# First attention of a four-layer kernel: the next pair's projections and values inside this pair's key tiles, and cross maxima in row tiles

## The reference, cut to what matters

```
# layer 0: first attention, 16 heads of 64
q = layernorm(x) @ Wq * 64 ** -0.5
k, v = split(media @ Wkv)                         # media: 1601 x 128
attn = softmax(where(mask, q @ k.T, min))         # 256 x 1601 for each head
x = x + tanh(attn_gate) * ((attn @ v) @ Wo)
x = x + tanh(ff_gate) * (gelu(layernorm(x) @ W1) @ W2)
# layer 1: memory attention; layer 2: self attention, cross attention, MLP
cq = rms_norm(h) @ cq_w; ck, cv = split(ctx @ ckv_w)   # 16 heads of 8
h = h + (softmax(cq @ ck.T / sqrt(8)) @ cv) @ cdense_w
# layer 3: memory attention
```

## Time and profile before

| | us |
|---|---|
| median of 3 runs | 2678.3 (2676.37 to 2683.85) |
| the profiled execution, its own time | 2683.99 |
| its span, first to last instruction | 2682.2 |
| one batch (start of one to start of the next) | 665.5 |

### The profile page before, as it was taken

One profiled execution on the slowest core, in us unless ns is written; L12 is line 12 of the kernel. 1 busy time (PEld: TensorE's weight loads), 2 busy tenths in 40 slices (PEclk: granted clock), 3 DMA queues, 4 the chain that ended last, 5 costly groups with the idle time before them and its releaser, 6 DMA issues.

```text
span 2682.2 us, 37982 instructions
## 1 busy us (share of the span) xinstructions
PE 2143.2 (80%) x12540; PEld 1575.9 (59%) x12540; DVE 1572.0 (59%) x2513; ACT 851.2 (32%) x1530; POOL 467.2 (17%) x412
## 2 busy tenths in 40 slices
PE   4999776878599977687859997768876999686987
PEld 3677565546477666554747766655464776565545
DVE  6777346653677735665377763566437776355643
ACT  2444111441244412054124441205412443120531
POOL 2444010000244401000034440100003443010000
PEclk7999877899699988798969998869896999886988
DMA  4000101001000010100100001010011000101000
GB/s 153 13 4 32 67 1 71 1 1 40 30 9 4 32 67 1 71 1 1 40 29 9 4 32 67 1 71 1 1 40 30 9 4 32 67 1 71 1 1 4
DMA packets 15563, 74.54 MB, mean 28 GB/s; under 512 B 2096, under 2 KB 3760, under 8 KB 11952
## 3 DMA queue, kind: packets, MB, share of 16 engines
q1 hardware_dynamic: 14256, 68.90, 6.9%
q10 hardware_dynamic: 1152, 3.67, 0.3%
HBM read 71.51 MB, written 1.05 MB: 27 GB/s over the span
## 4 chain that ended last, share of the span: by engine, by line
PE 72%; DVE 17%; issue 7%; ACT 3%; DMA 1%; POOL 0%; DVEq 0%; SPq 0%; ACTq 0%; POOLq 0%
PE x L623 26%; PE st L623 22%; PE pv L623 18%; PE mi L623 4%; DVE rstd_work L1142 1%; DVE prob_sums L1425 1%; DVE max_parts L1245 1%; PE x L642 1%; DVE k_hi_lo L1142 1%; DVE recip_sum L1296 1%; DVE cq_blocks L1480 1%; DVE rstd_work L1201 1%; ACT probs L508 1%; ACT k_hi_lo L466 1%; DVE max_parts L1472 1%
## 5 line engine op out<-in xcount | busy, mean ns | idle before, releaser
L508 ACT ACTIVATE probs<-st 128x512 f32<-128x512 f32 x416 | 229.6, 596 | 385.3 <-PE st L623 380.6
L1472 DVE TENSOR_REDUCE max_parts<-x 128x1 f32<-128x832 f32 x256 | 253.8, 1021 | 109.2 <-PE x L623 107.6
L1245 DVE TENSOR_REDUCE max_parts<-x 128x1 f32<-128x832 f32 x256 | 258.7, 1017 | 54.6 <-PE x L623 53.2
L602 ACT ACTIVATE probs<-st 128x512 f32<-128x512 f32 x416 | 226.3, 596 | 189.0 <-PE st L623 186.4
L623 PE MATMUL st<-q_hi_hi,k_hi_lo 128*128 128x256 f32 x832 | 236.8, 315 | 28.9 <-ACT v L474 14.3
L431 POOL TENSOR_TENSOR prob_sums<-prob_sums,probs 128x512 f32<-128x512 f32 x160 | 205.6, 1285 | 250.0 <-ACT probs L508 250.0
L623 PE MATMUL pv<-probs,v 128*64 128x256 f32 x1664 | 223.2, 393 | 0.0
L623 PEld LDWEIGHTS st<-q_hi_hi,k_hi_lo 128*128 128x128 f32 x832 | 160.7, 193 | 104.2 <-issue 68.4
L623 PE MATMUL st<-q_lo_shift,k_hi_rows 128*128 128x256 f32 x832 | 213.1, 287 | 0.0
L395 POOL TENSOR_SCALAR k_hi_rows<-probs,const_cols 64x1664 fp32r<-64x1664 f32 x16 | 26.4, 1658 | 996.1 <-DVE probs L1209 995.8
L1142 DVE TENSOR_TENSOR prob_sums<-prob_sums,probs 128x512 f32<-128x512 f32 (+1 forms) x168 | 155.2, 924 | 75.0 <-ACT probs L528 42.9
(11 more groups left out here) (260 smaller groups left out, 4405.8 us busy)
## 6 DMA issues: line engine op xcount, KB each, us to landing
w_gate_up<-in_wgu SPq DMA_DIRECT2D x4, 3072.0 KB, 10.5
w_pair<-in_w SPq DMA_DIRECT2D x32, 256.0 KB, 2.7
w_ff<-in_w SPq DMA_DIRECT2D x8, 1024.0 KB, 5.8
w_qk<-in_wqk SPq DMA_DIRECT2D x4, 2048.0 KB, 9.1
w_down<-in_wdn SPq DMA_DIRECT2D x4, 1536.0 KB, 13.8
w_dense<-in_wd SPq DMA_DIRECT2D x4, 1024.0 KB, 12.5
mask_ints<-in_mask SPq DMA_DIRECT2D x4, 832.0 KB, 4.6
ctx_t_raw<-in_ctxT SPq DMA_DIRECT2D x4, 832.0 KB, 6.2
```

The costliest lines, as they stand in the source:

```text
L508: act.activation(prob[:, kt % 4], ST[kt % 2][:], ACT.Exp, scale=HD0 ** -0.5).then_inc(p_exp.handle, 1)
L602: act.activation(prob[:, n % 4], ST[n % 2][:], ACT.Exp, scale=float(HC2) ** -0.5)\
L1245: dve.tensor_reduce(mxs[:, qt, h, half:half + 1], X[half][:].rearrange("p (c n) -> p c n", c=2)[:, :, 0:QUART], AX.XY, ALU.max).then_inc(m ...
L1472: dve.tensor_reduce(mxs[:, qt, h, half:half + 1], X[half][:].rearrange("p (c n) -> p c n", c=2)[:, :, 0:QUART], AX.XY, ALU.max).then_inc(m ...
```

## The change

- `prep_q` and `prep_k` of pair p + 1 (not p + 2) are issued inside pair p, behind the scores of key tiles 0 to 3. Only pair 0 is prepared ahead of the loop.
- The values of two pairs (a "duo") are made at once: the moving operand has 256 columns, a `prep_v` tile is two key tiles into `MI`, there are 7 of them per duo. Four lie in the even pair and three in the odd pair ahead of the duo. The first duo's are made ahead of the loop.
- The maximum parts move from key tiles 2 to 9 to tiles 4 to 11, half 0 of the keys first. The transposed maxima go through `MI`.
- The sum of exponentials and the normalisation of pair p move behind the first two score tiles of pair p + 1. ScalarE copies `PV` to `attn` first (a new operation of 128 x 256), VectorE then multiplies in SBUF.
- VectorE adds three times per pair (tiles 5 and 7, 9, 11) instead of six tiles in five additions, GpSimd eight times instead of six.
- The pairs are written out instead of looped; the weights of a pair come in one buffer of 3 x 128 columns plus one of 256 columns per duo.
- In the second cross attention a maximum part is two heads x 416 keys instead of one head x 832 keys, and its two matmuls use only the 32 rows of their head.

The core of the diff (`...` marks what is left out; the ScalarE, GpSimd and SyncE parts follow the same order):

```diff
+DUOS = PAIRS // 2
+VT = -(-KT // 2)
+VS = 4
+ADD_DVE = (5, 7, 9, 11)
+ADD_POOL = tuple(kt for kt in range(KT) if kt not in ADD_DVE)
...
+        def v_tile(p, k0):
+            if p >= PAIRS - 2 or k0 < 2:
+                return None
+            c = k0 // 2 - 1 if p % 2 == 0 else VS + k0 // 2 - 1
+            return (p // 2 + 1, c) if c < (VS if p % 2 == 0 else VT) else None
...
@@ block.gpsimd: pair
+                    for n, kt in enumerate(ADD_POOL[1:]):
+                        pool.wait_ge(p_exp.handle, p_exp.at(i, kt + 1))
+                        if n == 0:
+                            pool.wait_ge(sum_mm.handle, sum_mm.at(i, 0))
+                            pool.tensor_tensor(acc[:, 0], prob[:, 0], prob[:, 1], ALU.add).then_inc(add_pool.handle, 1)
...
+                                queries(i + 1, 1 - p % 2)
+                                keys(i + 1, 1 - p % 2, 0)
...
+                        if kt == 3 and p < PAIRS - 1:
...
+                            keys(i + 1, 1 - p % 2, 1)
@@ block.scalar: pair
+                    for k0 in range(0, KT, 2):
+                        for kt in range(k0, min(k0 + 2, KT)):
+                            probs(kt)
+                        if p < PAIRS - 1 and k0 == 0:
+                            queries(i + 1, 1 - p % 2)
+                            keys(i + 1, 1 - p % 2, 0)
+                        if p < PAIRS - 1 and k0 == 2:
+                            keys(i + 1, 1 - p % 2, 1)
+                        if v_tile(p, k0):
+                            values(*v_tile(p, k0), MI)
+                    act.wait_ge(pv_mm.handle, pv_mm.at(i))
+                    act.activation(attn[:, p], PV[:, 0:NT], ACT.Copy).then_inc(pv_out.handle, 1)
@@ block.tensor: pair
                     for k0 in range(0, KT, 2):
                         for kt in range(k0, min(k0 + 2, KT)):
                             scores(kt)
-                        if not last_pair and 2 <= k0 < 10:
-                            max_part(i + 1, 1 - s, k0 - 2)
-                            max_part(i + 1, 1 - s, k0 - 1)
+                        if k0 == 0 and p:
+                            sums(i - 1)
+                        if p < PAIRS - 1:
+                            if k0 == 0:
+                                prep_q(i + 1, 1 - s, False)
+                                prep_k(i + 1, 1 - s, 0)
+                            if k0 == 2:
+                                prep_k(i + 1, 1 - s, 1)
+                            if v_tile(p, k0):
...
+                                prep_v(c, MI)
+                            if 4 <= k0 < 12:
+                                max_part(i + 1, 1 - s, k0 - 4)
+                                max_part(i + 1, 1 - s, k0 - 3)
                         if k0:
                             pv(k0 - 2)
                             pv(k0 - 1)
                     pv(KT - 1)
-                    if not last_pair:
-                        shifts(i + 1)
-                    if more:
-                        prep_q(i + 2, s, None)
-                        prep_v(i + 2, s, 0, None)
-                        prep_k(i + 2, s, None)
...
+                        shifts(i + 1)
@@ block.tensor: cross_max
-                    for ch in range(2):
-                        o = half * HALF + ch * QUART
-                        m = mm(X[half][:, ch * 512:ch * 512 + QUART], qb2[gr % 2][:, h, qt * P:(qt + 1) * P], ks2[gr % 2][:, o:o + QUART])
+                    for u in range(2):
+                        h = 2 * duo + u
+                        r = slice(32 * h, 32 * h + 32)
+                        m = mm(X[duo][:, u * 512:u * 512 + QUART], qb2[gr % 2][r, h, qt * P:(qt + 1) * P],
+                               ks2[gr % 2][r, c * QUART:(c + 1) * QUART])
@@ block.vector: pair
+                    if p:
+                        normalise(p - 1)
+                    if more:
+                        queries(i + 1, 1 - s)
+                        keys(i + 1, 1 - s, 0)
+                        if p < PAIRS - 2:
+                            split(p + 2)
+                        keys(i + 1, 1 - s, 1)
+                        max_part(i + 1, 0)
+                        max_part(i + 1, 1)
+                    add(7)
+                    if more:
+                        max_part(i + 1, 2)
+                        max_part(i + 1, 3)
+                    add(9)
+                    if more:
+                        for n in range(4, 8):
+                            max_part(i + 1, n)
                         neg_max(i + 1)
+                    add(11)
...
```

More of the change, by code:

```diff
@@ L439, in _ @@
+                        if kt == 3 and p < PAIRS - 1:
+                            pool.wait_ge(add_pool.handle, add_pool.at(i, n + 1))
+                            keys(i + 1, 1 - p % 2, 1)
+                for p in range(PAIRS):
+                    pair(p)
                 pool.wait_ge(gate_mm.handle, gate_mm.at(b * 2))
@@ L459, in _, with queries @@
             with act.Fori(0, B) as b:
[L460 to L473, removed]
-                        act.activation(t["v"][:, k0:k1].rearrange("p k n -> p (k n)"), ST[j % 2][:, 0:(k1 - k0) * P], ACT.Copy)\
-                            .then_inc(v_read.handle, 1)
+                def queries(i, s):
@@ L477, in prep @@
                     act.wait_ge(q_mm.handle, q_mm.at(i))
                     for h in range(2):
-                        act.activation(t["qx"][0:64, h], MI[64 * h:64 * h + 64, 0:NT], ACT.Copy).then_inc(q_hi.handle, 1)
-                    if p is None:
-                        values(0)
-                    keys(0)
-                    keys(1)
-                    for j in range(0 if p is not None else 1, 4):
-                        values(j)
+                        act.activation(par[s]["qx"][0:64, h], MI[64 * h:64 * h + 64, 0:NT], ACT.Copy).then_inc(q_hi.handle, 1)
@@ L489, in _, with pair, probs @@
                 act.activation(cth[:], craw[:], ACT.Copy).then_inc(cth_ready.handle, 1)
-                prep(b * PAIRS, 0, 0)
+                queries(b * PAIRS, 0)
+                keys(b * PAIRS, 0, 0)
+                keys(b * PAIRS, 0, 1)
+                for c in range(VT):
+                    values(0, c, ST[c % 2])
                 act.wait_ge(types_read.handle, types_read.at(b))
-                prep(b * PAIRS + 1, 1, 1)
-                def step(b, p, s, more, last):
+                def pair(p):
                     i = b * PAIRS + p
-                    for kt in range(KT):
+                    def probs(kt):
                         act.wait_ge(st_mm.handle, st_mm.at(i, kt + 1))
@@ L691, in prep_v @@
+                def prep_v(c, bank):
+                    for kt in range(2 * c, min(2 * c + 2, KT)):
+                        o = (kt % 2) * 2 * P
+                        for n, (w, x) in enumerate(((wvhi, cth), (wvlo, cth), (wvhi, ctl))):
+                            last = mm(bank[:, o:o + 2 * P], x[:, kt * P:(kt + 1) * P], w[:], n == 0, n == 2)
                     last.then_inc(v_mm.handle, 1)
@@ new lines, in sums, with pair @@
+                def sums(i):
+                    pe.wait_ge(pv_out.handle, pv_out.at(i))
+                    pe.wait_ge(add_pool.handle, add_pool.at(i))
+                    pe.wait_ge(add_dve.handle, add_dve.at(i))
+                    for h in range(2):
+                        for k in range(2):
+                            m = mm(PV[64 * h:64 * h + 64, NT:2 * NT], ones[:, 0:64], acc[:, k, h * NT:(h + 1) * NT], k == 0, k == 1)
+                    m.then_inc(sum_mm.handle, 1)
+                def pair(p):
+                    i, s = b * PAIRS + p, p % 2
+                    t = par[s]
@@ L1028, in cross_max @@
                     i = b * 4 + gr
-                    half, h, qt = n % 2, n // 2 % 4, n // 8
+                    duo, c, qt = n % 2, n // 2 % 4, n // 8
                     if n < 2:
@@ L1264, in _ @@
                 tt(vmb[:, 0:NT - 1], rec[:, 0:NT - 1], rec[:, 1:NT], ALU.mult).then_inc(types_read.handle, 1)
-                prep(i0, 0)
-                prep(i0 + 1, 1)
+                queries(i0, 0)
+                keys(i0, 0, 0)
+                keys(i0, 0, 1)
                 for n in range(8):
@@ L1302, in _ @@
+                for p in range(PAIRS):
+                    pair(p)
+                normalise(PAIRS - 1)
                 dve.wait_ge(wo_mm.handle, wo_mm.at(b))
```

338 lines of the change are left out of this document (171 added, 167 removed).

## The result

The changed kernel takes 2710.2 us (median of 4 runs, 2706.6 to 2712.9) where the kernel before took 2681.1 in the same comparison: a ratio of 1.010 with the interval 1.009 to 1.012. It is slower by 1%; the forecast was 2611. The profiled execution's own time is 2709.2, its span 2707.4.

A forecast was written before the change was run, and what follows sets the result against it. TensorE was taken to bound pairs and cross key tiles, chain length the stretches ahead of pair 0 and in the first cross maxima. (-9.4 attention - 7.4 cross) x 4 = -67 from 2684.0 gives 2617, as median 2611 us; range 2570 to 2658.

The forecast's parts named there:

- the layout: First attention: one pair's engine timeline from its first score matmul; even pairs 26.9 us, odd pairs 26.4.
- one such hit: VectorE in each pair: one instruction, the weight split, delayed by GpSimd's running addition; 0.55 us seen in the trace before.
- the rule: VectorE and GpSimd share SBUF interfaces when VectorE's instruction has two SBUF inputs; up to five instructions a pair.
- a clock lost in the pairs' new stalls: First attention's pairs: named among other ways to be slower, without a size; chance 0.03 for these together.
- Pairs 0 to 5: First attention: six pairs take 160 us for 169.1, -9.2 a batch.
- Pair 6: First attention: now prepares pair 7 without value tiles to cover VectorE's chain; 25.4 us for 19.6, +5.8 a batch.
- Ahead of pair 0: Preparation before the loop: less work, first maximum part at about 715.3 instead of 722.11, -6.8 us a batch.
- The bare end: End of each pair: transposes, cast and next weight load stand alone, uncovered by preparation, 1.4 us.
- Cross maxima: Second cross attention in row tiles: two key tiles 3.3 us for 3.6; -5.0 and -2.4, sum -7.4 a batch.
- the bounds: Cross row tiles: from no overlap, +3.3 us a batch, to weight loads overlapped too, -11.5; nearest to column tiles taken.
- that rival: Cross key tiles: granted clock falls to its lower level, +34 us a batch, 2766 us in all; chance 0.05.
- The longer chain: Pairs: five VectorE instructions with two SBUF inputs each wait 0.7 us more for GpSimd; 2640 us; chance 0.17.

The follow-up runs named there:

- subtraction-only experiment: Changed kernel with only the weight split's subtraction moved behind the shifts at the pair's end, its copy left among the low keys: 2638.2 us, ratio 0.983.
- the split moved: Changed kernel with the whole weight split of pair p + 2 moved from between the low-key halves to behind the shifts: 2617.8 us, ratio 0.976.
- the covered end: Changed kernel with the weight split late, plus queries and key half 0 of pair p + 2 behind the shifts' transposes: 2614.5 us, ratio 0.974.

## Why the prediction was wrong

It was wrong in sign: -67 us forecast for the profiled execution, +25 measured. One term was too small, one that hangs on it was missing, and one sum of the layout was added up wrongly.

- **The weight split between the low keys: mis-sized.** The layout gives it 1.5 us, 8.2 to 9.7, with "one such hit" by GpSimd. It takes 3.0, because both instructions are hit, the copy by 1.0 us and the subtraction by 1.0. The stall at the second maximum part is 2.59 for the forecast 1.1: 1.5 more, term for term. I had seen GpSimd's addition meet the split once in the kernel before, and counted the meetings of before instead of laying GpSimd's own timeline beside the new one. There, the high-key copy for TensorE stands in front of the additions of tiles 2 and 3, so these come late and back to back, under the split.
- **The copy counted as free: a reading error.** I took the half of the rule that names two SBUF inputs. The subtraction-only experiment shows the copy held too. Its own rate gives it away: from 256 to 384 columns a copy grows by 0.07 (0.29 to 0.36), a subtraction by 0.14 (0.42 to 0.56), so the copy reads at twice the rate. The Trainium skill ("GPSIMD Engine Reference", Specifications) names both kinds, two SBUF inputs or a 2-port performance mode; the prediction quoted only the first. The Trainium skill ("SBUF — State Buffer", SBUF: two separate sides) has the shared pair of ports as an exclusive lock for the whole instruction. The rows agree in the main: the product of 0.42 that started 0.04 behind an addition of 1.31 ended at 797.29, 0.29 behind the addition's end, and where the product started first, GpSimd paid.
- **The clock behind the stall: missing.** The layout puts a stall of 1.1 in each pair and prices it at 1.1. The stall of 2.59 brought 1.5 more (the experiment with useless matmuls: 1.50). The prediction named "a clock lost in the pairs' new stalls" with a small chance and no price, while pricing the same loss for the cross tiles. The trace of before showed no such stall inside a pair, so the price was not to be read there, but both levels were.
- **Pairs 0 to 5.** Forecast 26.65, measured 30.35: 1.5 of stall, 1.5 of clock, and some 0.6 that is a slip of the sum. The layout's stretch from 11.8 on is 0.4 + 1.0 + 3 x 2.93 + 1.4 + 2.1 + 0.6 = 14.3, which ends at 26.1, not at 25.4; the 0.6 of waits was named and not added. Added, pairs are about 27.3 and the forecast 2625. With the split moved the stall is 0.9 less than in the layout, and pairs are 26.4, which is what 27.3 less 0.9 gives. So the layout of the pair was right but for this one place; that the whole kernel then comes to 2617.8, near the forecast 2611, is luck: there the stall of 1.1, which the forecast had, is nearly gone, and that hides the slip.
- **Pair 6.** Forecast 25.4, measured 27.4. Its stall was forecast as 2.4 and is 2.1; most of the rest is the clock again: 25.9 in the batch where the clock holds. Both stay when the split is moved, since there is none in this pair: there the clock is 0.90 in the 16.4 us behind the stall, 1.00 ahead of it.
- **Ahead of pair 0, pair 7, values.** -7.6 for -6.8; 0.0 for +0.8; a value matmul of 256 columns every 0.12, as taken (812.80 to 812.92).
- **The bare end** was there at every pair: 0.96 on the cast.
- **Cross maxima.** Two key tiles 3.34 for the forecast 3.3; 26.4 us by themselves for 4 x 7.4 = 29.6. The choice between the bounds (the neighbour in column tiles) held. The clock in the key tiles did not fall (1.00 in 1174 to 1192); that rival is out.
- **The longer chain** was the rival nearest to what happened, with the wrong list. Of its five instructions the split's subtraction (1.56 for 0.56) and the first two additions (1.1 to 1.4 for 0.69) were held, but not the product (0.42); the one that mattered beside the subtraction was a copy, on no list. And it had no clock in it: 37.6 us of clock are more than the +29 by which the kernel is slower, and without them (the experiment with useless matmuls) it is at 0.996 of the kernel before.

## What to carry to other kernels

Before a VectorE instruction is put on a critical chain, lay GpSimd's instructions beside its new place: an instruction with two SBUF inputs, and an SBUF copy at the doubled rate like the one here, may have to wait for the end of what GpSimd is doing, while the low keys, with one of their two inputs in PSUM, passed: half 1 took 2.06 also where two additions ran beside it (798.74, the split moved). Moving two such instructions by half a pair was worth 92 us here, and one product 39. And price a stall of TensorE twice: its length, and a fall of the clock that may follow, here 1.5 us. Which stalls it follows is not a matter of length alone. Behind the stalls of 0.96 between pairs, of 1.00 (only the subtraction moved) and of 1.47 (the covered end) inside them the clock fell not once in the whole execution. Behind 2.6 it fell 22 times in 24, and behind the same 2.12 of pair 6 three times in four in the changed kernel and with the split moved, and once in four with GpSimd's additions cut. What decides it for a given stall stays open.

## What the runs showed of the hardware

- A VectorE copy of 128 x 384 fp32 from SBUF to SBUF took 0.36 us alone and 1.37 to 1.41 beside a running GpSimd addition; a subtraction of the same size 0.56 and 1.54 to 1.56; two of GpSimd's additions beside them took 2.70 for 1.28 each alone. So the price was VectorE's. Where VectorE's instruction had started first, it kept its 0.42 and GpSimd's copy took 0.83 for 0.61.
- One fall of the granted clock was worth 1.5 us, both with 2.55 us of useless matmuls in the gap, which prevented it (37.6 us over 25 falls), and between two batches of one execution (pair 5: 30.15 at 0.94, 28.58 at 1.00).
- Covering a wait can uncover a collision: the preparation that filled TensorE's gap brought GpSimd's work forward in step with VectorE's product, and that gave the gain back until the product was moved.
